# A graph layer's last stage: VectorE forms the low halves one group ahead of its sums, and stores are issued two groups behind

## The chip, the cores and the metric

The kernel runs on one core of a Trainium2 chip. The metric is the device time of one launch in microseconds; the time before is the median of three runs. One further execution was profiled, and all rows below come from it.

## The reference

One layer of a graph network over 6250 nodes with 512 features and 100,000 edges. Cut to what matters:

```python
xn = layernorm(x)
x = x + gnn(xn, src, dst) + linear_attention(xn)       # stages before the last ones
t = layernorm(x)
hs = gelu(einsum('td,nfd->ntf', t, sw1) + sb1)          # 2 shared experts, 256 hidden
shared = einsum('ntf,ndf->td', hs, sw2) + sb2.sum(0)
cw = top-2 of softmax(t @ gate_w.T + gate_b)            # 2 of 8 routed experts per node
routed = einsum('etd,te->td', routed_experts(t), cw)
return x + shared + routed
```

The changed stage computes `shared` and adds it to `x` and to the two weighted rows of `routed`.

## The kernel before

The program is written engine by engine: each engine has its own instruction list, in the order of the code, and engines meet only at semaphores. The order of an engine's list is therefore the order of its work; nothing reorders it. There are several stages. The routed experts' rows are computed in the stage ahead of the last one and stored in the DRAM tensor `yd`; the nodes' values `x2d` and their normalised, transposed form `x2t` lie in DRAM too.

The last stage goes over NG = 25 groups of 250 nodes (G = 2 halves of T = 125). Two buffers of each kind are used in turn, b = group mod 2; there are 2 shared experts, e = 0 and 1. Precise float32 products are had from float16 matmuls: each operand is split in a high and a low half, and three products are summed. So a hidden activation has to exist as a high half `hTd[e][:, 0]` (ScalarE) and a low half `hTd[e][:, 1]` (VectorE) before TensorE may use it.

For group i the work is:

- SyncE loads `x2t` (500 KB, `load_turned`, line 534) and `x2d` (512 KB, `load_x2`, line 539). Its list is: both loads of groups 0 and 1, then turned(2), x2(2), turned(3), x2(3), and so on. turned(i) waits for the buffer to be free, that is until TensorE has done the hidden products of group i - 2 (`d_f1`). x2(i) waits until VectorE has done the last result of group i - 2 (`d_res`), whose sums use the same buffer `acc[b]`. turned(i + 1) stands behind x2(i) in the list.
- GpSimd gathers the four sets of rows of `yd` (line 735), once VectorE's sums of group i - 2 are done (`d_y`, line 727).
- TensorE: `hidden_shared(i, b, e)` (lines 1420 to 1422, 24 matmuls) and `project_shared(i, b, e)` (lines 347 to 349 called from 1433, 12 matmuls). Its order is hidden(i, 0), project(i-1, 1), hidden(i, 1), project(i, 0). hidden(i, 0) waits for turned(i) (line 1414). project(i, e) waits for both halves (`d_hi`, `d_lo`, lines 1426 and 1427), and project(i, 0) also for the results of group i - 2 (line 1430).
- ScalarE: the two gelus of an expert (line 1018) and then its high half (line 1023). The high half of group i waits for project(i-1, 1) (`d_f2`, line 1022), since `hTd` is single per expert. The store of group i - 1 stands between the work of expert 0 and expert 1 of group i (line 1012).
- VectorE: `combine(i, b)`. It first makes both low halves of group i (line 2132), then adds the shared bias to the loaded `x2d` (line 2136), adds the four weighted routed rows (line 2143) and at last the two PSUM results of project(i, 1) (line 2149), with `d_res`. Ahead of the first `combine` it waits for the two shared bias rows, which GpSimd loads at the start of the stage (line 723), and adds them (line 2126).

Of the kernel before, what the change touches and what calls it, by code (L numbers as in the profile page):

```python
# [6 lines left out]
ALU = mybir.AluOpType  # L7
# [14 lines left out]
NG = NT // G  # L22
# [6 lines left out]
NE, FE = 8, 256  # L29
# [30 lines left out]
def gps_layer_kernel(nc, x, edges, dst_flat, w_kv, w_q, w_sn, w_out, w_gate, w_1, w_2, b_1, b_2, rows, gate_b, out):  # L60
# [8 lines left out]
    with ExitStack() as ctx:  # L69
# [21 lines left out]
        sem = {n: ctx.enter_context(nc.semaphore(n)) for n in names}  # L91

        def pair(name):
            return [sem[name + "0"], sem[name + "1"]]
# [110 lines left out]
        def carve(region, n, dt=F32, parts=128):  # L205
            words = n if dt == F32 else n // 2
            v = region[0:parts, at[0]:at[0] + words]
            at[0] += words
            assert at[0] <= region.shape[1]
            return v if dt == F32 else v.bitcast(dt)  # L210
# [68 lines left out]
        sb2 = carve(region2, 2 * D, parts=T).rearrange("p (j n) -> p j n", j=2)  # L279
# [3 lines left out]
        def two(b):  # L283
            return bank[b][:, 0:2 * GT].rearrange("p (c n) -> p c n", c=2)
# [66 lines left out]
        def past(i):  # L351

            return not isinstance(i, int) or i > 0
# [396 lines left out]
        def _(act):  # L750
# [252 lines left out]
            def store(i, b):  # L1003
                act.wait_ge(sem["d_res"], 2 * i + 2)
                rows = out[bass.ds(i * GT, GT), :].rearrange("(j p) n -> p j n", j=G)
                act.dma_start(rows[0:T16], res[b][0:T16]).then_inc(pair("d_out")[b], 16)
                act.dma_start(rows[T16:T], res[b][T16:T]).then_inc(pair("d_out")[b], 16)

            def shared(i, b):
                for e in range(NS):  # L1010
                    if e and past(i):
                        store(i - 1, 1 - b)
                    act.wait_ge(sem["d_f1"], 2 * i + e + 1)
                    if past(i):
                        act.wait_ge(sem["d_lo"], 2 * i + e - 1)
                    for c in range(2):
                        f = 2 * e + c
                        act.activation(geld[e][:, c, :], two(e)[:, c, :], ACT.Gelu, bias=b1[:, f:f + 1],
                                       scale=sv[:, S_W1:S_W1 + 1]).then_inc(sem["d_gelu"], 1)
                    act.wait_ge(sem["d_gelu"], 4 * i + 2 * e + 2)  # L1020
                    if past(i):
                        act.wait_ge(sem["d_f2"], 2 * i)
                    act.activation(hTd[e][:, 0], geld[e], ACT.Copy, scale=sg[:, HB:HB + 1]).then_inc(sem["d_hi"], 1)

            act.wait_ge(sem["x2_out"], 16 * NG)
            act.wait_ge(sem["rows2_out"], 16 * NG)
            act.wait_ge(sem["x2t_out"], 16 * NG)
            shared(0, 0)
            shared(1, 1)
            with act.Fori(1, NG // 2) as m:  # L1030
                for b in range(2):
                    shared(2 * m + b, b)
            shared(NG - 1, 0)
            store(NG - 1, 0)


# [427 lines left out]
        def _(dve):  # L1464
            tt, ts, stt = dve.tensor_tensor, dve.tensor_scalar, dve.scalar_tensor_tensor
# [596 lines left out]
            a, b, d, n = KA, KB, 1, 7  # L2062
            while d < NE + 1:
# [3 lines left out]
                a, b, d, n = b, a, 2 * d, n + 2  # L2067
# [54 lines left out]
            made(b2bc[:, NE - 1, :], hi)  # L2122


            dve.wait_ge(sem["b2_in"], 16 * NE + 32)
            tt(sb2[:, 0, :], sb2[:, 0, :], sb2[:, 1, :], ALU.add).then_inc(sem["sb2_sum"], 1)
            dve.wait_ge(sem["sb2_sum"], 1)

            def combine(i, b):
                for e in range(NS):  # L2130
                    dve.wait_ge(sem["d_hi"], 2 * i + e + 1)
                    stt(hTd[e][:, 1], geld[e], sg[:, HB:HB + 1], hTd[e][:, 0], ALU.mult, ALU.subtract).then_inc(sem["d_lo"], 1)  # L2132

                x2b = acc[b][0:T]
                dve.wait_ge(pair("dx_in")[b], 8 * (i - b) + 16)
                tt(x2b, x2b, sb2[:, 0:1, :].broadcast_to([T, G, D]), ALU.add).then_inc(sem["sb2_sum"], 1)
                dve.wait_ge(pair("yg_in")[b], 32 * (i - b) + 64)
                dve.wait_ge(sem["sb2_sum"], i + 2)
                for k in range(2):
                    for j in range(G):  # L2140
                        if k:
                            dve.wait_ge(sem["d_y"], 4 * i + j + 1)
                        stt(x2b[:, j, :], yr[b][0:T, j, k, :], wcur[b][:, 2 * j + k:2 * j + k + 1], x2b[:, j, :], ALU.mult, ALU.add).then_inc(sem["d_y"], 1)
                for j in range(G):
                    dve.wait_ge(sem["d_y"], 4 * i + 3 + j)
                    dve.wait_ge(sem["d_f2"], 2 * i + j + 1)
                    if past(i - b):
                        dve.wait_ge(pair("d_out")[b], 16 * (i - b))
                    stt(res[b][0:T, j, :], bank[2 + 2 * b + j][0:T, :], sv[0:T, S_W2:S_W2 + 1], x2b[:, j, :], ALU.mult, ALU.add).then_inc(sem["d_res"], 1)

            combine(0, 0)
            combine(1, 1)
            with dve.Fori(1, NG // 2) as m:
                for b in range(2):
                    combine(2 * m + b, b)
            combine(NG - 1, 0)

# [47 lines left out]
```

## Time and profile before

| what | us |
|---|---|
| median of three runs (lowest, highest) | 2157.23 (2155.22, 2158.01) |
| the profiled execution: its own time | 2157.89 |
| the profiled execution: its span | 2156.3 |
| last stage in the span | about 1881 to 2156 |
| TensorE busy over the whole span | 2012.7 (93%) |
| VectorE, ScalarE, GpSimd busy | 1524.0, 1070.1, 1274.1 |

The span is what the trace covers, from its first instruction to its last; the execution's own time is 1.6 us longer. Busy shares are averages over stages with different limits, so the stage that is changed has to be read by itself. The granted clock is given as a share of TensorE's full clock of 2.4 GHz: 1.00 is 2.4 GHz and 0.50 is 1.2 GHz. "Idle before" is the time for which an engine did nothing ahead of an instruction, with what ended it behind the arrow.

### The profile page before, as it was taken

The numbers are of one execution on the slowest core, as the hardware profiler recorded it, in microseconds if no ns is written. First come the engines' busy times: TensorE is split into PE (matmuls) and PEld (weight loads), VectorE is DVE, ScalarE is ACT, GpSimd is POOL, SyncE is SP. The second block draws the span as 40 slices with busy tenths as digits, with TensorE's granted clock in tenths as the row PEclk, the third lists the DMA queues.
The fourth block names the chain that finished last, engine by engine and source line by source line (L and its number), as shares of the span: only waits on it lengthen the run. The fifth ranks groups of instructions, "written<-read, shape, count | busy, mean of one in ns | idle before, by whom it ended". The sixth has DMA issues, their size and how long they took to land. (4 is left out here: it accounts for less than half of the span.)

```text
span 2156.3 us, 47156 instructions
## 1 busy us (share of the span) xinstructions
PE 2012.7 (93%) x12724; PEld 1356.5 (63%) x12725; DVE 1524.0 (71%) x3774; ACT 1070.1 (50%) x2102; POOL 1274.1 (59%) x1360
## 2 busy tenths in 40 slices
PE   5999997999999999999999999995799999889998
PEld 2555554666666666666666666663577777667776
DVE  7888885668887787877888787886344444356666
ACT  3555774645546565565645555452344444323332
POOL 3666776777777777777777777760233333153442
PEclk9999998999999999999999999997799999999999
DMA  8855646788888888888888888874455555567765
GB/s 294 271 163 171 247 163 174 226 257 265 261 266 270 259 255 259 264 256 258 256 260 268 252 258 259 262 236 166 146 166 175 170 167 170 165 218 259 256 241 203
DMA packets 187677, 492.47 MB, mean 228 GB/s; under 512 B 41357, under 2 KB 54157, under 8 KB 185833
## 3 DMA queue, kind: packets, MB, share of 16 engines
q0 software_dynamic: 91920, 306.84, 47.0%
q1 hardware_dynamic: 65929, 135.51, 18.1%
q10 hardware_dynamic: 29775, 49.51, 6.7%
q8 instruction: 22, 0.36, 0.1%
q14 instruction: 31, 0.25, 0.0%
HBM read 371.29 MB, written 120.41 MB: 228 GB/s over the span
## 5 line engine op out<-in xcount | busy, mean ns | idle before, releaser
L692 POOL DMA_INDIRECT region<-table,idx x112 | 110.2, 984 | 289.6 <-DMA region<-table,idx 203.9
L642 POOL DMA_INDIRECT region<-table,ebuf x225 | 216.5, 962 | 78.4 <-issue 78.1
L642 POOL DMA_INDIRECT Wff<-table,ebuf x225 | 215.5, 958 | 75.3 <-issue 68.3
L347 PE MATMUL bank<-Wff,region 128*125 128x512 f16 (+2 forms) x620 | 238.7, 385 | 13.4 <-DVE region L2132 7.5
L653 POOL DMA_INDIRECT Wff<-table,ebuf x200 | 210.1, 1050 | 60.9 <-issue 60.9
L348 PE MATMUL bank<-Wff,region 128*125 128x512 f16 (+2 forms) x620 | 237.4, 383 | 0.0
L349 PE MATMUL bank<-Wff,region 128*125 128x512 f16 (+2 forms) x620 | 237.2, 383 | 0.0
L653 POOL DMA_INDIRECT region<-table,ebuf x200 | 198.6, 993 | 61.0 <-issue 60.4
L1189 PE MATMUL bank<-region,ohs 128*125 128x512 f16 x850 | 190.8, 382 | 5.2 <-DMA region<-table,ebuf 5.2
L1189 PE MATMUL bank<-Wff 128*125 128x512 f16 x850 | 191.5, 384 | 0.4 <-DMA Wff<-table,ebuf 0.4
L871 ACT ACTIVATE region<-bank,dg 125x512 f32<-125x512 f32 x50 | 34.4, 687 | 271.7 <-DVE counted L1794 211.3
L1189 PEld LDWEIGHTS bank<-region,ohs 128*125 128x125 f16 x850 | 114.5, 138 | 70.7 <-DMA region<-table,ebuf 7.0
L1189 PEld LDWEIGHTS bank<-Wff 128*125 128x125 f16 x850 | 115.3, 138 | 65.9 <-issue 2.8
L347 PE MATMUL bank<-Wsn,region 128*125 128x512 f16 x400 | 152.9, 382 | 1.1 <-DVE region L1946 1.0
L349 PE MATMUL bank<-Wsn,region 128*125 128x512 f16 x400 | 151.5, 379 | 0.0
L348 PE MATMUL bank<-Wsn,region 128*125 128x512 f16 x400 | 151.5, 379 | 0.0
L861 ACT ACTIVATE Wff<-iota_f,ebuf 128x125 f16<-128x125 f32 x425 | 125.8, 386 | 28.0 <-issue 28.0
L2100 DVE SCALAR_TENSOR_TENSOR region<-bank,sv,region 128x512 f32<-128x512 f32 x110 | 82.3, 751 | 71.5 <-PE bank L349 60.0
L2093 DVE COPY region<-bank 128x1024 f16<-128x1024 f16 x56 | 38.7, 692 | 130.2 <-PE bank L1363 130.2
L861 ACT ACTIVATE ohs<-iota_f,ebuf 128x125 f16<-128x125 f32 x425 | 125.8, 386 | 7.3 <-DMA ebuf<-edges 2.8
L735 POOL DMA_INDIRECT region<-yd,yi x100 | 100.7, 1007 | 42.2 <-issue 22.9
L1374 PE MATMUL bank<-region,Wff 128*128 128x256 f16 x440 | 121.8, 277 | 2.0 <-DVE region L2093 1.9
(328 smaller groups left out, 5461.9 us busy)
## 6 DMA issues: line engine op xcount, KB each, us to landing
yd<-region ACTq DMA_DIRECT2D x55, 512.0 KB
x2d<-region SPq DMA_DIRECT2D x25, 512.0 KB
table<-region SPq DMA_DIRECT2D x25, 512.0 KB, 4.4
region<-x2d SPq DMA_DIRECT2D x25, 512.0 KB, 5.0
table<-region POOLq DMA_DIRECT2D x50, 250.0 KB, 3.7
xnt<-region POOLq DMA_DIRECT2D x25, 500.0 KB, 4.0
region<-xnt SPq DMA_DIRECT2D x25, 500.0 KB, 4.5
x2t<-region SPq DMA_DIRECT2D x25, 500.0 KB
```

Source lines behind the costliest of these rows:

```text
L347: wmm(ps, xh, wh, start=first, stop=False)
L348: wmm(ps, xh, wl, start=False, stop=False)
L349: return wmm(ps, xl, wh, start=False, stop=last)
L642: pool.indirect_dma_start(out=ring[j][:, s, :], out_offset=None, in_=table, in_offset=bass.IndirectOffsetOnAxis(ap=ebuf[j][:, 2 * s:2 * s ...
L653: pool.indirect_dma_start(out=ring[j][:, s, :], out_offset=None, in_=table, in_offset=bass.IndirectOffsetOnAxis(ap=ebuf[j][:, 2 * s:2 * s ...
L692: pool.indirect_dma_start(out=tg[:, turn, c, :], out_offset=None, in_=table2, in_offset=bass.IndirectOffsetOnAxis(ap=idx[:, 2 * turn + c:2 ...
L735: pool.indirect_dma_start(out=yr[b][:, j, k, :], out_offset=None, in_=yd, in_offset=bass.IndirectOffsetOnAxis(ap=yi[b][:, 2 * j + k:2 * j ...
L861: act.activation(oh[j][:, s, :], iota_f[:], ACT.Abs, bias=ebuf[j][:, 2 * s + 1:2 * s + 2], scale=-1.0).then_inc(made_in, 1)
L1189: last = wmm(bank[6][0:T, :], oh[j][:, s, :], ring[j][:, s, part * D:(part + 1) * D], start=False, stop=False, skip_group_check=True)
L1374: wmm(ps, w1(e, 0, k, c), tTc[:, 0, k, :], start=(k == 0), stop=False)
L2093: dve.tensor_copy(tTc[:, :, :, 128:256], parts16(3, 128)).then_inc(sem["ct_dve"], 1)
L2100: stt(ysb[:, j, :], bank[4 + j][:, :], sv[:, S_W2:S_W2 + 1], bias, ALU.mult, ALU.add).then_inc(sem["y_sb"], 1)
```

## The change

VectorE's two low halves leave `combine` and become `low_shared(i)`. It is called for groups 0 and 1 ahead of the shared bias sum, and then for group i + 1 ahead of `combine(i)`. ScalarE's store of a group is issued one group later, inside the work of group i for group i - 2, and two stores are left for the end. SyncE's, GpSimd's and TensorE's lists stay as they are.

```diff
             def shared(i, b):
                 for e in range(NS):
-                    if e and past(i):
-                        store(i - 1, 1 - b)
+                    if e and past(i) and past(i - 1):
+                        store(i - 2, b)
...
             shared(NG - 1, 0)
+            store(NG - 2, 1)
             store(NG - 1, 0)
...
-            dve.wait_ge(sem["b2_in"], 16 * NE + 32)
-            tt(sb2[:, 0, :], sb2[:, 0, :], sb2[:, 1, :], ALU.add).then_inc(sem["sb2_sum"], 1)
-            dve.wait_ge(sem["sb2_sum"], 1)
-
-            def combine(i, b):
+            def low_shared(i):
                 for e in range(NS):
                     dve.wait_ge(sem["d_hi"], 2 * i + e + 1)
                     stt(hTd[e][:, 1], geld[e], ...).then_inc(sem["d_lo"], 1)
 
+            def combine(i, b):
                 x2b = acc[b][0:T]
...
+            low_shared(0)
+            low_shared(1)
+            dve.wait_ge(sem["b2_in"], 16 * NE + 32)
+            tt(sb2[:, 0, :], sb2[:, 0, :], sb2[:, 1, :], ALU.add).then_inc(sem["sb2_sum"], 1)
+            dve.wait_ge(sem["sb2_sum"], 1)
             combine(0, 0)
+            low_shared(2)
             combine(1, 1)
             with dve.Fori(1, NG // 2) as m:
                 for b in range(2):
+                    low_shared(2 * m + b + 1)
                     combine(2 * m + b, b)
             combine(NG - 1, 0)
```

## Rows read from the trace of the kernel before

**Rows 1.** Windows: length, busy time (count) of PE, PEld, DVE, ACT, POOL, clock, DMA.

```profile
1880.00:1900.00 20.00, 12.48 (x73) 8.48 (x72) 5.77 (x8) 3.44 (x6) 8.48 (x12) 0.74 0.46 140
1900.00:2144.00 244.00, 244.00 (x1708) 186.38 (x1706) 161.54 (x213) 80.91 (x141) 101.14 (x140) 1.00 0.71 247
```

**Rows 2.** Timeline of TensorE: start, us, what, idle before; first matmuls of blocks.

```profile
1894.10 0.66 PE L347 MATMUL bank<-Wff,region 128*125 128x512 f16 x1 [7.52 <-DVE region L2132]
...
1904.60 0.27 PE L1420 MATMUL bank<-region,Wff 128*128 128x250 f16 x1
...
1909.76 0.27 PE L1420 MATMUL bank<-region,Wff 128*128 128x250 f16 x1
...
1914.93 0.27 PE L1420 MATMUL bank<-region,Wff 128*128 128x250 f16 x1
...
2136.88 0.27 PE L1420 MATMUL bank<-region,Wff 128*128 128x250 f16 x1
```

**Rows 3.** Timeline of ScalarE: the first high half.

```profile
1885.17 0.71 ACT L1023 ACTIVATE region<-region,sg 128x500 f16<-128x500 f32 x1
```

**Rows 4.** Timeline of VectorE: start of the stage, groups 1 and 2, end.

```profile
1892.48 0.69 DVE L2126 TENSOR_TENSOR region<-region 125x512 f32<-125x512 f32 x1 [10.26 <-DMA region<-b]
...
1919.49 0.74 DVE L2132 SCALAR_TENSOR_TENSOR region<-region,sg 128x500 f16<-128x500 f32 x1 [2.82 <-ACT region L1023]
1920.14 1.22 DVE L2136 TENSOR_TENSOR region<-region 125x1024 f32<-125x1024 f32 x1
1921.40 2.74 DVE L2143 SCALAR_TENSOR_TENSOR region<-region,wcur 125x512 f32<-125x512 f32 x4
1924.32 0.75 DVE L2149 SCALAR_TENSOR_TENSOR region<-bank,sv,region 125x512 f32<-125x512 f32 x1 [0.18 <-DVE region L2143]
...
2151.24 1.40 DVE L2149 SCALAR_TENSOR_TENSOR region<-bank,sv,region 125x512 f32<-125x512 f32 x2
```

**Rows 5.** Timeline of SyncE's DMA queue: start of an issue, its us, what.

```profile
1860.28 0.43 SPq L539 DMA_DIRECT2D region<-x2d  x1
1860.76 0.42 SPq L534 DMA_DIRECT2D region<-x2t  x1
...
1916.11 0.33 SPq L539 DMA_DIRECT2D region<-x2d  x1
1917.95 0.34 SPq L534 DMA_DIRECT2D region<-x2t  x1
```

**Rows 6.** Waits of SyncE's queue, from 1876: total us, times, longest.

```profile
SPq L539 <- DVE region L2149: 195.6, 23, 18.2
```

**Rows 7.** DMA issues in the last stage: size, median us from issue to landing.

```profile
region<-x2d SPq DMA_DIRECT2D x23, 512.0 KB, 5.0
region<-yd,yi POOLq DMA_INDIRECT x100, 6.4
```

**Rows 8.** Line 534, all 25 loads of `x2t`: us from issue to landing.

```profile
DMA to landing us min/median/max: 3.8/7.0/8.1
```

**Rows 9.** Landings of the loads issued at 1860.28, 1860.76 and 1861.23.

```profile
DMA to landing us min/median/max: 6.8/6.8/6.8
...
DMA to landing us min/median/max: 8.1/8.1/8.1
...
DMA to landing us min/median/max: 10.0/10.0/10.0
```

**Rows 10.** DMA queues from 1951.5 to 1955.5: packets, MB, share of 16 engines.

```profile
q0 software_dynamic: 233, 0.77, 48.6%
q1 hardware_dynamic: 145, 0.51, 31.2%
```

**Rows 11.** Timeline of TensorE in earlier stages: three gaps and what follows.

```profile
387.74 2.59 PE L1189 MATMUL bank<-region,ohs 128*125 128x512 f16 x11 [1.94 <-DMA region<-table,ebuf]
...
432.01 2.39 PE L1189 MATMUL bank<-region,ohs 128*125 128x512 f16 x5 [2.27 <-DMA region<-table,ebuf]
...
1870.09 2.35 PE L1363 MATMUL bank<-ident,region 128*128 128x128 f16 x16 [3.17 <-DMA region<-table,idx]
```

**Rows 12.** Windows behind the gap at 432.

```profile
434.00:435.00 1.00, 1.00 (x3) 0.46 (x2) 0.00 (x0) 0.00 (x0) 0.69 (x2) 0.50 0.88 224
435.00:436.00 1.00, 1.00 (x5) 0.64 (x4) 0.00 (x0) 0.00 (x0) 0.70 (x2) 0.84 0.83 130
```

## The prediction

> **What bounds the kernel now.** I read the stage windows first. From 1900 to 2144 us TensorE is busy for all of 244 us at the full clock of 2.4 GHz, so no other engine bounds the steady part of the last stage. Only at its start is there time to win: from 1880 to 1900 it is busy 12.48 of 20 us, at a mean granted clock of 0.74 [rows 1]. The timeline of TensorE gives the place: 7.52 us idle ahead of project(0, 0), ended by VectorE's first low half [rows 2]. VectorE in turn had waited 10.26 us for the bias rows in front of line 2126 [rows 4], though the high half that it needed was there at 1885.17 + 0.71 = 1885.88 [rows 3].
>
> The pace comes from the first matmuls of the blocks: 1904.60, 1909.76, 1914.93 [rows 2]. A group of four blocks takes 10.33 us and a block 2.58. I call H(i) the start of hidden(i, 0). Before, H(2) = 1909.76 and H(24) = 2136.88, where 22 groups of 10.325 give 227.1.
>
> **The start: what is won.** The first low half no longer stands behind the bias rows. It can follow 1885.88 at once, takes 0.74, and TensorE starts about 0.15 behind it (1893.95 to 1894.10 before): about 1886.8 instead of 1894.10, 7.3 us. Behind the idle time the clock was at 0.50. From 1894.10 to 1904.60 three blocks took 10.5 instead of 7.74 [rows 2]: 2.75 us more, also won, since no gap longer than a few tenths is left there. H(2) comes 10.0 us earlier, at 1899.7. The bias rows and their sum now lie beside TensorE's blocks and cost nothing; uncovered the sum would cost its 0.69 [rows 4].
>
> **The steady part: what the move of the low halves delays.** No instruction is added in the loop. But on VectorE combine(i) now stands behind the second low half of group i + 1, which needs hidden(i + 1, 1), gelu and high half. Group 1 and 2 of before give the times. hidden(2, 1) starts at 1914.93 and the low half behind it begins at 1919.49 [rows 2, 4]. From there the sums need 1920.14 to 1924.14 (bias sum and four row sums), 0.18 of wait, and 1.40 for two results by the last pair [rows 4]: the end is at 1925.72, 10.8 us behind 1914.93. Since H(2) lies 5.17 ahead of 1914.93, results of group i are done at H(i + 1) + 15.95. Before, they were done near H(i + 1) + 6.2, right behind project(i, 1). VectorE itself stands it: its next low half is wanted at about H(i + 1) + 16.45, half a microsecond later, and TensorE needs that at +18.1.
>
> What does not stand it is SyncE's list. It waits on VectorE's results at x2(i + 2) and has always waited there: 195.6 us in 23 waits [rows 6]. Behind that wait is turned(i + 3), and hidden(i + 3, 0) needs it. Before, x2d was issued at 1916.11, 0.2 behind the results, and x2t 1.84 later, landing 7.0 after its issue (about 1925), against a need at H(4) = 1930.4: 5 us of slack. Now both are issued some 9.8 us later against the same need. In numbers: results of group i at H(i + 1) + 15.95; x2d issue 0.18 later; x2t right behind (0.48 in the pair at 1860.28 and 1860.76 [rows 5]); landed X us after the x2d issue; and hidden(i + 3, 0) is wanted at H(i + 1) + 20.65. The load is in time only if X is at most 4.5.
>
> X is not seen in this arrangement. The nearest rows: x2d alone lands 5.0 after issue [rows 7], and behind a first load the next ones land 1.8 to 3.6 us apart: issues at 1860.28, 1860.76 and 1861.23 with 6.8, 8.1 and 10.0 us give landings at 1867.1, 1868.9 and 1871.2, with the first x2t at 1863.5 (3.8) [rows 8, 9]. So X is 6.8 to 8.6. The quickest single landing, 3.8, and 1.8 behind it give 5.6 as lower end. In one period x2t's packets, half a MB, went out in some 3 us beside the gathers [rows 10]; started 0.5 us behind x2d's, with the same gathers and the store still to move, they end about 2 us behind them. I take X = 7.0, near the low end of what the pair shows, as the bursts are otherwise the same ones.
>
> The Trainium skill, "DMA: Bandwidth & Descriptors", section "Queues, rings and completion order", says that an engine consumes one ring in order and changes between queues packet by packet. Three queues (loads, store, gathers) would by an even share give x2t a third of what moves, and X would come out nearer to 8.6 than to 7.
>
> Then H(i + 3) = H(i + 1) + 15.95 + 0.18 + 7.0 = H(i + 1) + 23.1 against 20.65: 2.5 us of stall per two groups. It is a loop (load, three blocks, low half, sums, load), so the loss does not get absorbed, it recurs. The first time is group 3: results of group 0 are at H(1) + 15.95 + 0.7 = 1889.4 + 16.65 = 1906.05, x2t lands at 1913.2, wanted at 1910.0: 3.2 us. H(4) then follows 10.33 behind H(3), for its own load is in time by then, and H(5), H(7) to H(23) stall again, ten times 2.5. Together 28.2 us. Odd groups stall and even ones do not.
>
> **The clock behind the stalls.** A gap of 1.94 us left the clock full (eleven matmuls in 2.59 us), one of 2.27 put it to 0.50 (five matmuls in 2.39), and 3.17 did too [rows 11]. Behind the 2.27 it was at 0.50 until about 435.3 [rows 12], some 3.3 us from 432.0: 1.7 lost. The gap of 7.52 in this stage cost 2.75. Eleven stalls of 2.5 to 3.2 lie just above the one that fell. I take that the clock falls to 1.2 GHz behind seven of them, at 1.8 us each: 12.6 us. It lies on the loop as well, since three blocks follow each stall. Bounds: none (0) and all at 2.75 (30 us).
>
> **Stores and the end.** The store of group i - 2 waits for results that are there about when ScalarE reaches it (its high half ends at H(i - 1) + 16.45, the results at +15.95): no wait for gelu, cost nothing; with results late by more it would hold the gelu of expert 1, which has about 1 us. A result buffer is wanted two groups later, far behind any landing. The gathers start with the sums and land about 12 us later (6.4 from issue [rows 7]) against 19: no wait. At the end the sums of group 23 no longer lie beside TensorE. Before: H(24) = 2136.88 to 2156.3, 19.4 us. Now: 15.95 to the results of group 23, then combine(24) with 5.6, then 3.66 from the last result (2152.64) to the end: 25.2. That is 5.8 us more. The extra store lands beside combine(24).
>
> **Sum**, against the profiled execution's 2157.9 (span 2156.3 and 1.6 around it): -10.0 + 28.2 + 12.6 + 5.8 = +36.6, so 2194.5. The median is 0.7 below that execution: 2194.
>
> **Rivals.**
> (A) The same stalls, but the clock stays up, as behind the gap of 1.94: -10.0 + 28.2 + 5.8 = +24, 2181. Against it is the gap of 2.27.
> (B) The clock falls behind every stall at 2.75: +54, 2211. For it is that all gaps from 2.27 up fell; against it that the one of 2.27 cost 1.7 only. The Trainium skill, "TensorE: Matmul & The Clock Gate", section "HAM oscillation — how this bites in real kernels", describes a kernel whose clock falls at every wait for a load; this trace has no such series of gaps.
> (C) The loads are in time: x2t does not queue behind x2d and lands 4.0 after its own issue, as it does in quiet (3.8 [rows 8]). Then the stage keeps its pace: -10.0 + 5.8 = -4.2, 2153. It decides at X = 4.5. Against it: in the stage's bursts even x2d, first in the queue, takes 5.0.
> (D) X is 5.6, a short stall: 1.1 in each of ten and 1.8 first, 13 us, gaps too short for the clock: +9, 2166.
> (E) X is 8.6: stalls of 4.1, 46 us in all, and the clock falls each time by 2: +64, 2221.
>
> **How the numbers follow.** The forecast has 0.47, A 0.20, B 0.12, C 0.08, D 0.07, E 0.06. A run of this kernel can be told from no change at about 0.2%, 4.3 us. C lies on that bound and is split: faster 0.05, within 0.2% 0.04, with 0.91 slower. The likeliest case itself spans 2186 to 2203 (four to ten falls, X 6.8 to 7.3). The range of 2172 to 2211 takes in A and B and leaves out C, D and E.
>
> **What would show it.** Right: TensorE idle ahead of line 1420, ended by the DMA of x2t, about eleven times, at every second group, 2.5 us each; the waits of SyncE's line 534 gone and its issue right behind line 539; granted clock under 1.00 in the steady windows; H(2) near 1899.7; the last row sums behind each other with TensorE done. It would be wrong if no wait on x2t shows (C), if the idle time is ended by a low half of VectorE instead, or if the stalls sit at all groups.

## The result

| | before | changed |
|---|---|---|
| median us (lowest to highest) | 2156.22 (2154.84 to 2158.01) | 2200.31 (2196.9 to 2203.73) |
| span of the profiled execution | 2156.3 | 2195.2 |
| last stage: first hidden matmul to the end of the span | 2156.3 - 1881.3 = 275.0 | 2195.2 - 1880.5 = 314.7 |

The ratio is 1.0203, with a 95% interval of 1.019 to 1.0216: slower by 44 us in the median, against 37 forecast, inside the stated range. The profiled execution of the changed kernel is the fastest of its four. Its span is 38.9 us longer, and the last stage alone is 39.7 longer, so the whole loss lies there.

The windows of the changed kernel, in the columns of [rows 1]:

```profile
1880.00:1900.00 20.00, 19.78 (x145) 15.25 (x144) 5.23 (x8) 6.89 (x12) 9.06 (x13) 1.00 0.50 149
1900.00:2180.00 280.00, 245.08 (x1644) 182.93 (x1643) 152.54 (x206) 78.97 (x138) 98.20 (x139) 0.97 0.60 210
```

The start that had 7.5 us of idle time is now full, at the full clock. The steady part that was full has lost 35 us of 280. The waits name the place; the first row is TensorE's, the others are those of SyncE's queue (total us, times, longest):

```profile
PE bank L1421 <- DMA region<-x2t: 34.9, 11, 3.5
```

```profile
SPq L539 <- DVE region L2147: 260.2, 23, 18.5
SPq L534 <- PE bank L1423: 24.8, 2, 24.6
```

SyncE's wait at line 539 grew by 65 us against [rows 6], and line 534 (x2t) has no wait of its own left beyond the first of 24.6: whenever it is reached, its buffer has long been free. TensorE's timeline shows the pattern; five of the eleven stalls:

```profile
1912.93 0.38 PE L1421 MATMUL bank<-region,Wff 128*128 128x250 f16 x1 [3.50 <-DMA region<-x2t]
1938.34 0.28 PE L1421 MATMUL bank<-region,Wff 128*128 128x250 f16 x1 [3.15 <-DMA region<-x2t]
1962.34 0.28 PE L1421 MATMUL bank<-region,Wff 128*128 128x250 f16 x1 [3.18 <-DMA region<-x2t]
...
2035.86 0.39 PE L1421 MATMUL bank<-region,Wff 128*128 128x250 f16 x1 [3.19 <-DMA region<-x2t]
2061.29 0.28 PE L1421 MATMUL bank<-region,Wff 128*128 128x250 f16 x1 [3.19 <-DMA region<-x2t]
```

The distances between stalls are 24.0 us (1938.34 to 1962.34) or 25.4 (2035.86 to 2061.29), against 20.65 for two groups before. SyncE's queue, to be read against [rows 5]:

```profile
1954.20 0.33 SPq L539 DMA_DIRECT2D region<-x2d  x1
1954.83 0.33 SPq L534 DMA_DIRECT2D region<-x2t  x1
```

From the issue at 1954.20 to the stall's end at 1962.34 are 8.1 us: that is X, with the 0.2 us from the landing to the first matmul in it. It is 7.6 at the first stall and 7.9 to 8.2 at the others.

Where the 39.7 us are, from the trace:

| term | forecast | measured |
|---|---|---|
| start (where group 3 is wanted: 28.9 behind the stage's first matmul, 38.8 before) | -10.0 | -9.9 |
| stalls, eleven | +28.2 | +34.9 |
| end (last start of line 1421, before 1420, to the end of the span: 17.2, before 12.0) | +5.8 | +5.2 |
| what is left, forecast as TensorE at 1.2 GHz behind stalls | +12.6 | +9.5 |

### The profile page after: what moved, and what is told of

Its sections match the earlier page's. It is cut to its first block and busy times, and to the rows that moved or that the text cites. A ratio compares the mean times of both kernels' runs of the same rounds, so it can differ in the third digit from the quotient of the medians.

```text
span 2195.2 us, 47178 instructions
## 1 busy us (share of the span) xinstructions
PE 2018.8 (92%) x12724; PEld 1358.2 (62%) x12725; DVE 1519.8 (69%) x3774; ACT 1070.7 (49%) x2102; POOL 1275.9 (58%) x1360
## 5 line engine op out<-in xcount | busy, mean ns | idle before, releaser
L1421 PE MATMUL bank<-region,Wff 128*128 128x250 f16 x400 | 111.8, 279 | 34.9 <-DMA region<-x2t 34.9
L1018 ACT ACTIVATE region<-bank,b,sv 128x250 f32<-128x250 f32 x100 | 50.5, 556 | 178.0 <-PE bank L1423 178.0
L2129 DVE SCALAR_TENSOR_TENSOR region<-region,sg 128x500 f16<-128x500 f32 x50 | 36.9, 739 | 141.5 <-ACT region L1023 141.5
```

The costliest lines, as they stand in the source:

```text
L1421: wmm(ps, w1(NE + e, 0, k, c), tTd[b][:, 0, k, :], start=(k == 0), stop=False)
```

## The experiments

"Stage" is, as above, from the first hidden matmul to the end of the span, in the profiled execution. The stages ahead of it differ by several us between executions, so the stage tells more than the whole time.

**x2t ahead in SyncE's list (e1).** In the changed kernel:

```diff
+            load_turned(2, 0)
             with sp.Fori(0, (NG - 3) // 2) as m:
                 for b in range(2):
-                    load_turned(2 * m + b + 2, b)
+                    load_turned(2 * m + b + 3, 1 - b)
                     load_x2(2 * m + b + 2, b)
-            load_turned(NG - 1, 0)
             load_x2(NG - 1, 0)
```

> The changed kernel, with one edit in SyncE's list alone: x2t of group i+1 is issued ahead of x2d of group i, so it no longer stands behind SyncE's wait for VectorE's results. My theory (the whole steady loss is x2t queued behind that wait): all eleven stalls of 2.9 to 3.5 us and the clock falls behind them go, the start's 10 us stay won and the end's 6 us stay lost: about 2153, between 2150 and 2156. Rival (VectorE's new order itself, or the load on the DMA engines, bounds the stage): TensorE still waits in most groups and the time stays above 2175.

Measured: 2152.11, ratio 0.9978 (0.9968 to 0.9987), stage 270.2. Its steady window, in the columns of [rows 1]:

```profile
1885.00:2130.00 245.00, 245.00 (x1713) 187.07 (x1711) 154.92 (x209) 81.52 (x143) 107.24 (x147) 1.00 0.72 245
```

No idle time and no fall of the clock are left. VectorE's order, which is the change, is the same as in the slow kernel. So it does not bound the stage; the place of x2t behind the wait does. The stage is 4.8 us shorter than before, where start and end alone give 4.7.

**Only the first low halves moved (e2).** The kernel before, with the low halves of group 0 ahead of the bias sum:

```diff
+            low_shared(0)
             dve.wait_ge(sem["b2_in"], 16 * NE + 32)
...
             def combine(i, b):
-                (the two low halves)
+                if past(i):
+                    low_shared(i)
```

> The kernel before, with only the two low halves of group 0 moved ahead of the bias rows' sum; the order of all other groups and the stores as before. My theory: the gap of 7.5 us and the 2.75 us at 1.2 GHz behind it go, nothing comes in their place: about 2146. Rival (the start's gain is met by another wait, for instance for the gathered rows or for the next x2t, since these do not come earlier): 2151 to 2156.

Measured: 2154.29, ratio 0.9993 (0.9983 to 1.0002), stage 273.9: the rival. The first gap is gone, but VectorE and TensorE show the next one:

```profile
1890.88 2.74 DVE L2147 SCALAR_TENSOR_TENSOR region<-region,wcur 125x512 f32<-125x512 f32 x4 [3.63 <-DMA region<-yd,yi]
```

```profile
1895.68 0.66 PE L347 MATMUL bank<-Wff,region 128*125 128x512 f16 x1 [5.85 <-issue]
```

VectorE stands 3.63 us in combine(0) until the gathered rows land, and only behind it comes the low half of group 1 (its row starts at 1894.85), for which TensorE waits at project(1, 0). The profile calls that gap "issue"; the low half, which ends at 1895.58, is what it ends with. The first matmul is at half the clock again (0.66 us). The bias rows were the first late thing, the gathered rows of group 0 the next.

**x2t first, same wait (e3).** The changed kernel; SyncE waits for VectorE's result, then issues x2t and behind it x2d:

```diff
+            load_turned(2, 0)
             with sp.Fori(0, (NG - 3) // 2) as m:
                 for b in range(2):
-                    load_turned(2 * m + b + 2, b)
-                    load_x2(2 * m + b + 2, b)
-            load_turned(NG - 1, 0)
+                    sp.wait_ge(sem["d_res"], 2 * (2 * m + b + 2) - 2)
+                    load_turned(2 * m + b + 3, 1 - b)
+                    load_x2(2 * m + b + 2, b, False)
```

> The changed kernel, with SyncE still waiting for the same result of VectorE ahead of both loads, but x2t of group i+1 issued first and x2d of group i behind it. It tells the late issue from the place in the queue. If the place behind 512 KB of x2d makes half of the 8.1 us, x2t lands some 4.2 us after its issue, as x2d does now in that place, just under the 4.6 at which a stall begins: 2150 to 2158. If the share of the DMA engines sets the landing whatever the place, it takes 6 to 7 us and stalls of 1.5 to 2.5 us remain: 2175 to 2190.

Measured: 2156.44, ratio 1.0001 (0.9992 to 1.0011), stage 277.8. There is one gap, 4.79 us at group 3, and none behind it. The landings of x2t from 1930 on:

```profile
DMA to landing us min/median/max: 4.3/4.4/4.7
```

This is just under what two groups leave: 20.65 - 15.7 - 0.2 = 4.8. So in the steady part the late issue does no harm if x2t goes first. X of the changed kernel is 8.1 because of what goes before it.

**Stores later, nothing else (e4).** The kernel before with the change's two edits of ScalarE.

> The kernel before with only the stores issued one group later. All theories that put the loss on the loads expect no change: 2156, within 4 us. If the later stores, which then compete with other transfers, were part of the loss, it would be over 2160.

Measured: 2154.84, ratio 0.9994 (0.9985 to 1.0004), stage 275.3. No change, as expected.

**The old order for the last groups (e5).** e1, and in VectorE's list:

```diff
-            with dve.Fori(1, NG // 2) as m:
+            with dve.Fori(1, NG // 2 - 1) as m:
                 ...
+            low_shared(NG - 2)
+            combine(NG - 3, 0)
+            combine(NG - 2, 1)
+            low_shared(NG - 1)
             combine(NG - 1, 0)
```

> The changed kernel with x2t ahead of x2d in SyncE's list, as before, and with VectorE's old order for the last two groups: the sums of groups 22 and 23 come before the low halves of group 24. My theory of the end (the sums of group 23 lie behind the low halves of group 24 and no longer beside TensorE, 5.8 us): about 2147, some 6 us under the run with the new end. Rival (the end is bound by its stores, not by VectorE): 2151 to 2155, like the run with the new end. A third way: two groups of sums in a row make the low half of group 24 late, some 4 us at TensorE, 2151.

Measured: 2150.02, ratio 0.9973 (0.9962 to 0.9983), stage 268.6, 1.6 under e1's instead of 6 (2.1 in the medians). The third way holds: two groups of sums in a row make the low half of group 24 late.

```profile
2141.45 0.61 PE L347 MATMUL bank<-Wff,region 128*125 128x512 f16 x1 [3.58 <-issue]
```

**The wait alone, in the kernel before (e6).**

```diff
             def load_x2(i, b, used=True):
                 if used:
+                    sp.wait_ge(sem["d_f2"], 2 * i)
                     sp.wait_ge(sem["d_res"], 2 * i - 2)
```

> The kernel before with one wait added in SyncE's list: x2d of group i, and so x2t of group i+1 behind it, is issued only when TensorE has finished project(i-1, 1), which is about when the changed kernel issues it (some 15.5 us behind the start of hidden(i-1, 0)). VectorE, ScalarE and stores stay as before. If the late issue alone makes the loss: eleven or so stalls of about 3 us and some clock falls, 2185 to 2200 (40 us over before, without the start's gain and the end's loss). If VectorE's new order is needed for the loss: 2156 to 2165.

Measured: 2256.75, ratio 1.0459 (1.0442 to 1.0477), stage 380.3: far over both. Its waits and three of its gaps:

```profile
PE bank L1421 <- DMA region<-x2t: 72.0, 22, 4.5
PEld bank L1421 <- DMA region<-x2t: 3.0, 1, 3.0
```

```profile
2045.60 0.28 PE L1421 MATMUL bank<-region,Wff 128*128 128x250 f16 x1 [2.42 <-DMA region<-x2t]
2060.01 0.28 PE L1421 MATMUL bank<-region,Wff 128*128 128x250 f16 x1 [3.91 <-DMA region<-x2t]
2073.77 0.28 PE L1421 MATMUL bank<-region,Wff 128*128 128x250 f16 x1 [3.27 <-DMA region<-x2t]
```

Every group from 3 on stalls, 22 times, not every second one. My expectation took the time of the event but not what it hangs on. VectorE's result of group i - 2 hangs on H(i - 1), so the loop of the changed kernel spans two groups. The end of project(i - 1, 1) hangs on H(i), one group closer: H(i + 1) is then at least H(i) + 5.2 + 0.2 + 8 = H(i) + 13.4 against 10.33, a stall of 3 us in each group. The experiment shows that a late issue, with VectorE's old order, is enough for stalls on x2t; it is no measure of the size in the changed kernel.

**Half of x2d ahead (e8).** The changed kernel, x2d in two loads of 256 KB with x2t of the next group between them.

> The changed kernel, with x2d loaded in two halves of 256 KB: first half (behind the same wait for VectorE's results), then x2t of the next group, then the other half. It is a dose between 512 KB ahead of x2t (stalls of 3.15 us) and none (no stall in the steady part). If the landing grows with the bytes ahead in SyncE's queue, x2t lands some 6.3 us behind the first issue: eleven stalls near 1.4 us, too short for the clock, 2165 to 2175. If it is all or nothing (the wait alone, or the share of other queues), stalls stay near 3 us, 2190 and more, or vanish, 2152 to 2157.

Measured: 2219.93, ratio 1.0297 (1.0279 to 1.0315), stage 343.2: fewer bytes ahead and yet longer stalls (3.6 to 5.2 us), with the clock at 1.2 GHz within a microsecond behind each of the eleven. The time lies on the "2190 and more" side of my expectation, but that side had stalls near 3 us; neither side named longer ones. The queues show a large part of it. Packets, MB and share of the engines, first in the changed kernel from 1957.2 to 1959.2 (3 to 5 us behind the issue of x2d at 1954.20):

```profile
q10 hardware_dynamic: 237, 0.45, 58.5%
q1 hardware_dynamic: 63, 0.19, 24.8%
q0 software_dynamic: 38, 0.16, 18.9%
```

and in this experiment from 1954.7 to 1956.7 (2 to 4 us behind the issue of the first half at 1952.70):

```profile
q10 hardware_dynamic: 240, 0.46, 66.7%
q1 hardware_dynamic: 68, 0.11, 17.2%
q0 software_dynamic: 29, 0.12, 15.3%
```

q10 is the store (500 KB), q1 is SyncE's queue. In both, nearly the whole store goes out between x2d and x2t, although x2t was issued only 0.5 us behind it. Half of x2d ahead buys nothing, since the store fills the place; the other half behind x2t then moves on q1 beside it, and x2t's stall ends at 1961.27, 8.6 us behind the first issue; at the other ten stalls these are 8.8 to 9.5 us, against some 8.1 in the changed kernel. That the second half is what adds this is argued from the queues; no run has x2d's second half out of the way. Of the 28.5 us that the stage is longer than in the changed kernel, 10 are longer stalls; most of the rest goes with the clock, which fell eleven times instead of five.

**The store out of the way (e10).** The changed kernel with the store behind both high halves:

```diff
-                    if e and past(i) and past(i - 1):
-                        store(i - 2, b)
...
                     act.activation(hTd[e][:, 0], geld[e], ACT.Copy, ...)
+                if past(i) and past(i - 1):
+                    store(i - 2, b)
```

> The changed kernel with each store issued some 3.5 us later still, behind both high halves of the group instead of between them; SyncE's list as changed. In the traces so far the store's packets go out between those of x2d and those of x2t, also when only half of x2d is ahead. My theory now (what holds x2t back is the store issued beside x2d, more than the bytes ahead in its own queue): x2t lands 1.5 to 2 us sooner, stalls of 1.2 to 1.7 us, too short for most clock falls, 2165 to 2178. Rival (all queues share one pool of moving time, the gathers take the place of the store): stalls stay at 2.8 us or more, 2190 to 2203.

Measured: 2184.9, ratio 1.0138 (1.0121 to 1.0155), stage 301.1, 13.6 us shorter than in the changed kernel; the median lies between the two expectations. x2t lands in 5.6 us (median) instead of 7.0. The gaps fall in two regimes:

```profile
1941.07 0.28 PE L1421 MATMUL bank<-region,Wff 128*128 128x250 f16 x1 [0.77 <-DMA region<-x2t]
1952.50 0.28 PE L1421 MATMUL bank<-region,Wff 128*128 128x250 f16 x1 [0.93 <-DMA region<-x2t]
...
2059.31 0.28 PE L1421 MATMUL bank<-region,Wff 128*128 128x250 f16 x1 [2.89 <-DMA region<-x2t]
2082.99 0.38 PE L1421 MATMUL bank<-region,Wff 128*128 128x250 f16 x1 [2.86 <-DMA region<-x2t]
```

Group 3 waits 1.9 us, and up to 1987 every further group waits 0.7 to 1.0, some 1.7 per two groups, where the theory had 1.2 to 1.7 at each second one; then every second group waits 2.7 to 2.9. So the store beside x2d is a part of X, shown; why the pattern turns over to long stalls in the second half is open.

**Two groups ahead, then the old order (e9).** The kernel before with the later stores (with the old ones, ScalarE's high half of group 1 would wait behind a store of group 0, and that for VectorE, for ever) and `low_shared(0)`, `low_shared(1)` ahead of the bias sum.

> The kernel before with the stores one group later and the low halves of groups 0 and 1, not only 0, ahead of the bias rows' sum; from group 2 on the order of before, SyncE's list as before. My theory (at the start the gathered rows of group 1 land too late for the old order, and VectorE stands in front of them while TensorE wants the low half of group 2): a gap of some 5 us now ahead of project(2, 0) and a fall of the clock, 2151 to 2156. Rival (only the wait behind the first gathered rows cost the gain): 2145 to 2148.

Measured: 2152.46, ratio 0.9983 (0.9973 to 0.9992), stage 271.8, 3.2 shorter than before. A gap ahead of project(2, 0) is there:

```profile
1911.31 0.68 PE L347 MATMUL bank<-Wff,region 128*125 128x512 f16 x1 [4.48 <-DVE region L2129]
```

Its cause is not the one that I expected. VectorE does not wait for the gathered rows of group 0 or 1 (line 2149 follows without idle time); the sums of both groups stand in a row ahead of the low halves of group 2, as in e5 at the end:

```profile
1901.07 2.74 DVE L2149 SCALAR_TENSOR_TENSOR region<-region,wcur 125x512 f32<-125x512 f32 x4
1903.73 1.40 DVE L2155 SCALAR_TENSOR_TENSOR region<-bank,sv,region 125x512 f32<-125x512 f32 x2
1905.05 1.21 DVE L2142 TENSOR_TENSOR region<-region 125x1024 f32<-125x1024 f32 x1
1906.36 2.74 DVE L2149 SCALAR_TENSOR_TENSOR region<-region,wcur 125x512 f32<-125x512 f32 x4
1909.02 1.40 DVE L2155 SCALAR_TENSOR_TENSOR region<-bank,sv,region 125x512 f32<-125x512 f32 x2
1910.34 1.38 DVE L2129 SCALAR_TENSOR_TENSOR region<-region,sg 128x500 f16<-128x500 f32 x2
```

**Changed order at the start, old order after it (e7).** e1 with VectorE's list in this order: changed order up to combine(3); first low half of group 5, combine(4), second low half of 5; bias sum of 5, first low half of 6, row sums of 5, second low half of 6, results of 5; from combine(6) on the order of before.

> The changed kernel with x2t ahead of x2d in SyncE's list, VectorE in the changed order for groups 0 to 3 only, then over groups 4 to 6 back to the order of before, in small steps that keep every low half in time. My theory: the start needs the changed order (the gathered rows come late there) and the end needs the old one, so the start's 10 us stay won and the end's 6 us are not lost: stage 10 us shorter than before, about 2146, the fastest of all. Rival (gathered rows hold the old order back as they did when only group 0 was moved): a gap of 2 to 5 us in TensorE near group 5, 2150 to 2153.

Measured: 2146.22, ratio 0.9955 (0.9941 to 0.9969), stage 267.1: the fastest version, 9 us under the kernel before (7.9 in the stage). One gap is left where the order is switched:

```profile
1959.24 0.42 PE L347 MATMUL bank<-Wff,region 128*125 128x512 f16 x1 [1.74 <-DVE region L2129]
```

**The same without the edit of SyncE's list (e11).**

> The fastest version with SyncE's list left as it was (x2d ahead of x2t): VectorE in the changed order for groups 0 to 3 only, then back to the order of before. My theory (each odd group in the changed order pays one stall): two stalls, at groups 3 and 5, of 3.5 and 3.2 us, and one or two falls of the clock at 1.7: 8 to 10 us over the fastest version, 2153 to 2157. Rival (the loop has to run for long to cost anything): 2146 to 2149.

Measured: 2154.7, ratio 0.9995 (0.9986 to 1.0005), stage 273.2: 8.5 us over e7 in the medians, 6.1 in the stage, and within 0.1% of the kernel before. The gaps:

```profile
1912.13 0.39 PE L1421 MATMUL bank<-region,Wff 128*128 128x250 f16 x1 [3.35 <-DMA region<-x2t]
1937.08 0.28 PE L1421 MATMUL bank<-region,Wff 128*128 128x250 f16 x1 [2.55 <-DMA region<-x2t]
1947.78 0.28 PE L1421 MATMUL bank<-region,Wff 128*128 128x250 f16 x1 [0.20 <-DMA region<-x2t]
```

Groups 3 and 5 pay a stall, group 6 almost none, and the loss stops when the order does.

## Why the prediction was right

- **The start.** -9.9 against -10.0. The gap and the half clock behind it went. What the prediction did not see is that the bias rows are not the only late thing: moving the low halves of group 0 alone wins 1.1 us in the stage and nothing clear of noise in the median (e2), and those of two groups 3.2 (e9). In e2 VectorE stands in front of the gathered rows of group 0, in e9 it has two groups of sums in a row; the changed order keeps each low half ahead of the sums and has neither gap. That the bias rows "lie beside TensorE's blocks and cost nothing" held together with that order.
- **The steady part.** The mechanism is the forecast one: x2t behind x2d behind VectorE's results, at odd groups, eleven times, a loop of two groups. e1 takes it away by SyncE's list alone. Results lie at H(i + 1) + 15.7 (1938.34 to 1954.0; forecast 15.95).
- **X was mis-sized.** 7.0 was forecast, 8.1 measured, within the bounds of 6.8 to 8.6. I had taken the low end, 5.0 for x2d and 2 behind it. x2d landed sooner (median 4.2 from 1930 on), x2t 3.6 us behind it at the load of 1954.20, and the store's half megabyte goes out between them. From its own issue x2t took 7.0 us in the median, as in the kernel before [rows 8]; that row and the 0.6 between the issues would have given 7.6. The prediction named the store as traffic and then treated "the same bursts" as if their order did not matter. The stalls came out 6.7 us longer in sum. X alone would make some 12. Results that lay 0.3 us earlier than forecast take 3 back; another 2 are 0.2 us at each stall that the idle time does not show and that stand in the table's last row.
- **The clock.** It fell behind five of eleven stalls here, not seven. From stall to stall it is 20.8 us (20.65 before) and the next stall where it stayed up, and 1.4 to 1.7 more where it fell: 7.7 us for the five. The rest of the 9.5 is the 0.2 us at each of the eleven stalls named above. So the term was too large in the number of falls and slightly in their price, and this cancels part of the error of X; that the sum comes so near is in part luck. The other executions of the changed kernel are 3 to 7 us longer at mean clocks of 0.974 to 0.976 against 0.977. Whether they had more falls is not shown, since the runs of e1, which has no stalls, also spread over 6.3 us.
- **The end.** +5.2 against +5.8. VectorE does 10.5 us of sums behind the last low half, those of group 23 and then those of group 24; they begin so:

```profile
2180.95 1.22 DVE L2134 TENSOR_TENSOR region<-region 125x1024 f32<-125x1024 f32 x1
2182.21 2.74 DVE L2141 SCALAR_TENSOR_TENSOR region<-region,wcur 125x512 f32<-125x512 f32 x4
2184.86 1.41 DVE L2147 SCALAR_TENSOR_TENSOR region<-bank,sv,region 125x512 f32<-125x512 f32 x2
2186.18 1.22 DVE L2134 TENSOR_TENSOR region<-region 125x1024 f32<-125x1024 f32 x1
```

- **The stores** cost nothing by their wait (e4), as said, but by the place of their packets (e10), which was not.
- Rival C (loads in time) is what e1 makes of the kernel: its -4.2 was measured as -4.8 in the stage.

## What to carry to other kernels

A step that is moved on one engine moves every event it signals: look up who waits for those, and what stands in that list behind the wait. Here the slow thing was no longer the sum that moved but an unrelated load behind it in an in-order list, and the repair is to issue the load whose buffer is free first. Before sizing a stall, ask on which earlier group the awaited event hangs, since that sets whether each group or each second one pays (e6), and which transfers were issued in between, since a landing time carries over only to the same place among the issues: x2t took 7.0 us behind x2d and a store, 5.6 without the store (e10) and 4.4 as the first (e3).

## What the runs showed of the hardware

**In this stage transfers went out nearly in the order of issue across queues.** A 500 KB store (448 KB issued 0.1 us behind x2d and 0.5 ahead of x2t, 52 KB beside x2t) was moved almost whole between them, with 512 KB or 256 KB of x2d ahead. x2t landed in 4.4 us as the first of its queue's burst (e3) and in some 7 as the last of three. The order is not strict: in e3 the store was issued within 0.05 us of x2t, both went out side by side, and x2t still landed in 4.4. The Trainium skill, "DMA: Bandwidth & Descriptors", section "Queues, rings and completion order", has each engine change between queues packet by packet; by an even share the store would not have passed so far ahead of x2t. The trace shows the packets' times and not since when x2t's were ready on the engines, so it does not tell whether the page's rule fails here or x2t's packets came late.

**The length of a gap does not settle whether the clock falls.** Windows of 3 us behind two stalls of the changed kernel, 3.18 and 3.19 us long; the granted clock is the first figure behind the counts:

```profile
1962.34:1965.34 3.00, 3.00 (x26) 2.62 (x27) 2.02 (x4) 0.15 (x1) 1.28 (x3) 1.00 0.10 36
```

```profile
2035.86:2038.86 3.00, 3.00 (x15) 2.19 (x16) 2.02 (x4) 0.00 (x0) 1.29 (x3) 0.51 0.09 33
```

Six stalls of 3.05 to 3.28 us left the clock at 2.4 GHz, five of 2.91 to 3.50 brought it to 1.2 GHz. In e6 it fell behind 16 of 22 stalls and stayed up behind six, one of them of 3.91 (2060.01). In the kernel before it fell behind 2.27 [rows 11]. So in the changed kernel a stall of such a length cost its own time and, in five of eleven cases, 1.4 to 1.7 us more.
